# Late weight pieces' transfers as steps of a hand-written order, and all three step lists laid anew

## The reference

```python
# graph convolution on _gn(x)                            steps of
prod = einsum(lhs(x), rhs(x));  E = softmax(V_e @ sigmoid(prod + b_e))     # M prod Epre Eexp Erep
prod2 = einsum(lhs2(x @ E), rhs2(x @ E))                                   # lr p2
S = softmax(V_s @ sigmoid(prod2 + b_s))                                    # sp rv
out = sum_k einsum(cheb[k], S, x) @ Theta[k]                               # Y st o
y = relu(conv1x3(relu(out), tw) + tb + einsum(x, rw) + rb)                 # tc
x = x + layernorm(y) * gamma + beta                                        # xb z1 z2 z3
# linear attention on _ln_t(t), causal, 16 heads
num = cumsum(phi(k) v^T) phi(q);  den = cumsum(phi(k)) . phi(q) + eps      # k q v S V, kt kv dent
t = t + (num / den) @ Wo.T + bo                                            # rd at wo
# mixture of experts on _ln_t(t): 16 experts of width 64, 2 of 4 groups, top 4, and a shared FFN of width 512
w = top4(sigmoid(xf @ router_w.T) + correction_bias);  w /= sum(w)         # lg r1 r2 r3 r4 cb
t = t + sum_e w_e * down_e(silu(gate_e xf) * up_e xf) + shared_ffn(xf)     # gu h w dn
```

## Time and profile before

| | us |
|---|---|
| three runs | 930.55, 930.71, 933.21 |
| median | 930.71 |
| the profiled execution | 933.24 |
| its span on the core | 931.3 |
| TensorE busy | 892.2 |
| VectorE busy | 623.1 |
| ScalarE busy | 445.6 |
| POOL busy | 228.6 |

### The profile page before, as it was taken

One profiled execution on the slowest core, in us unless ns is written; L12 is line 12 of the kernel. 1 busy time (PEld: TensorE's weight loads), 2 busy tenths in 40 slices (PEclk: granted clock), 3 DMA queues, 4 the chain that ended last, 5 costly groups with the idle time before them and its releaser, 6 DMA issues.

```text
span 931.3 us, 19454 instructions
## 1 busy us (share of the span) xinstructions
PE 892.2 (96%) x7824; PEld 787.5 (85%) x7824; DVE 623.1 (67%) x1637; ACT 445.6 (48%) x845; POOL 228.6 (25%) x198
## 2 busy tenths in 40 slices
PE   5998788999999999999999999999999999999997
PEld 3676666998988989889898989888898898998997
DVE  6456876887697468864797467963788547864522
ACT  3443444552574436743565526744466424732432
POOL 2013200123311224112421234112241134122232
...
DMA packets 37961, 39.21 MB, mean 42 GB/s; under 512 B 5232, under 2 KB 34416, under 8 KB 37872
## 3 DMA queue, kind: packets, MB, share of 16 engines
...
...
## 4 chain that ended last, share of the span: by engine, by line
PE 83%; DVE 8%; ACT 4%; issue 2%; DMA 1%; POOL 0%; SPq 0%; POOLq 0%; DVEq 0%; ACTq 0%
PE ring L1365 9%; PE d_ps L521 5%; PE g_ps L521 4%; PE d_ps L523 4%; PE d_ps L522 4%; PE g_ps L523 4%; PE u_ps L523 4%; PE g_ps L522 4%; PE u_ps L522 4%; PE u_ps L521 4%; PE ring L1233 4%; PE num L1262 3%; PE ring L521 3%; PE ring L1348 3%; PE ring L523 3%; PE ring L522 3%
## 5 line engine op out<-in xcount | busy, mean ns | idle before, releaser
L707 POOL TENSOR_TENSOR hl<-hb,hh 128x512 fp32r<-128x512 f32 x96 | 126.0, 1313 | 424.4 <-ACT hh L838 424.4
L838 ACT ACTIVATE hh<-hb 128x512 fp32r<-128x512 f32 x96 | 60.7, 632 | 143.5 <-DVE hb L1205 119.0
L1200 DVE TENSOR_TENSOR hb<-sl,u_ps 128x512 f32<-128x512 f32 x88 | 60.3, 685 | 93.3 <-issue 37.6
L521 PE MATMUL d_ps<-hh,down_h 128*128 128x256 f32 x384 | 116.6, 304 | 2.7 <-POOL hl L707 2.7
L522 PE MATMUL d_ps<-hl,down_h 128*128 128x256 f32 x384 | 107.8, 281 | 0.0
L523 PE MATMUL d_ps<-hh,down_l 128*128 128x256 f32 x384 | 107.6, 280 | 0.0
L521 PE MATMUL g_ps<-normed_h,gate_h 128*128 128x256 f32 x352 | 105.7, 300 | 1.1 <-DVE hb L1200 0.8
L1087 DVE TENSOR_TENSOR shared<-ring,constants 128x512 f32<-128x512 f32 x128 | 79.4, 683 | 34.1 <-PE ring L1233 34.1
L523 PE MATMUL g_ps<-normed_h,gate_l 128*128 128x256 f32 x352 | 99.2, 282 | 0.0
L523 PE MATMUL u_ps<-normed_h,up_l 128*128 128x256 f32 x352 | 99.0, 281 | 0.0
L522 PE MATMUL u_ps<-normed_l,up_h 128*128 128x256 f32 x352 | 98.8, 281 | 0.0
...
## 6 DMA issues: line engine op xcount, KB each, us to landing
weights_over_hidden<-weights_by_expert SPq DMA_DIRECT2D x128, 128.0 KB, 3.0
...
```

Of the source, the lines that this page charges most:

```text
L521: eng.matmul(ps, wh, xh, start=start, stop=False, **how)
L707: pool.tensor_tensor(hl[:, j % 2, :], hb, hh[:, j % 2, :].bitcast(F32), ALU.subtract).then_inc(*ffn_pool.mark(p, f"lo{j}"))
L838: act.activation(hh[:, j % 2, :], hb, ACT.Copy).then_inc(*ffn_act.mark(p, f"hi{j}"))
L1200: dve.tensor_tensor(hb, sl, gate_up(p, j)[1][:, :], ALU.mult).then_inc(*ffn_dve.mark(p, f"h{j}"))
```

## The change

The transfers of pieces 4 to 13 become steps load4 to load13 of a chain of their own. SP issues pieces 0 to 3 before its walk as before, and each later one where its step stands in the list; the wait for pair 1's z3 stays ahead of piece 4. All three lists are laid anew; the work in the steps is the same. Lines below the lists move by 2 to 8 (L1365 becomes L1373).

```diff
@@ -110,41 +110,43 @@
-ONCE = ("warm", "high", "low")
+EARLY_PIECES = 4
+CHAINS["load"] = [f"load{i}" for i in range(EARLY_PIECES, 14)]
+ONCE = ("warm", "high", "low", "load")
...
 OPENING = """
-    0:gn 0:hot0 0:xg 0:hot1 0:xT0 0:hot2 1:gn 0:M 0:xT1 0:high0 1:xg 0:high1 0:Y0 1:xT0 2:gn 0:high2 0:prod
...
+    0:gn 0:hot0 1:gn 0:hot1 0:xg 0:load4 1:xg 0:hot2 0:low0 0:high0 0:xT0 0:M 0:xT1 0:hot3 0:hot4 0:Y0 1:xT0
...
 BODY = """
-    +1 tok0 tok1 lg +1 gn +1 nrm +3 xg +1 r1 xl0 xl1 xT0 +1 r2 M +2 k0 xT1 k1 r3 +2 Y0 +1 prod v1 silu r4
-    Epre cb Eexp q0 v0 kt q1 +2 Erep dent +1 kv lr rd +2 S00 +2 V00 S01 +1 p2 at0 +1 V01 S10 +2 sp0 +1 rv0 +1
-    sp1 st0 +1 rv1 Y1 +2 st1 +1 o0 +2 V10 +1 S11 +2 o1 tc0 tc1 xb +1 z1 +1 V11 +2 at1 z2 +2 wo0 wo1 +2 tk0
-    exp tk1 +5 nrm2 z3 +1 xn0 xn1 +1
+    +1 tok0 tok1 lg +1 gn +2 nrm xg +1 r1 +3 xl0 xT0 xl1 M r2 +2 xT1 k0 k1 +2 Y0 +1 prod v1 r3 silu Epre r4
+    cb Eexp q0 v0 kt q1 +2 Erep dent kv +1 lr +1 rd +1 S00 +2 V00 S01 +1 p2 +1 at0 V01 S10 +2 sp0 rv0 sp1 +2
+    st0 +1 rv1 Y1 xb +2 st1 +1 o0 o1 +1 tc0 tc1 +2 z1 +2 V10 S11 +1 V11 +4 at1 z2 wo0 +1 wo1 +2 tk0 tk1 +2
+    nrm2 +3 z3 +1 xn0 xn1 +1 exp
 """
 
 CLOSING = """
...
-    7:r3 +1 7:silu 7:r4 +1 7:cb +30 7:exp +17
...
+    7:silu 7:r4 +1 7:cb +18 7:exp +32
@@ -546,7 +548,7 @@
 
         for half in (1, 0):
             feed_forward(gateT, gate_h, gate_l, 2 * wide, 0, half)
-        EARLY_PIECES = len(PIECES)
+        assert EARLY_PIECES == len(PIECES)
         for half in (1, 0):
             feed_forward(gateT, gate_h, gate_l, 2 * wide, 1, half)
             for k in range(2):
@@ -582,7 +584,11 @@
             for k in range(3):
                 sp.dma_start(cheb_s[:, k], cheb[k].rearrange("(c m) n -> m c n", m=P)).then_inc(load["graph"], 16)
             sp.dma_start(wo_s[:, :, :], woT.rearrange("(c j) k -> j c k", j=P)).then_inc(load["graph"], 16)
-            for i in range(len(PIECES)):
+            for i in range(EARLY_PIECES):
+                sp.dma_start(PIECES[i][3], PIECES[i][0]).then_inc(piece_loaded[i], 16)
+
+            def load_piece(i):
+
                 if i == EARLY_PIECES:
                     sp.wait_ge(tail_dve.of(1), tail_dve.at(1, "n30"))
                     sp.wait_ge(tail_pool.of(1), tail_pool.at(1, "n31"))
@@ -627,6 +633,8 @@
                                  source.unsqueeze(0).to_broadcast([64, 2, L])).then_inc(over_loaded[r % 2], 16)
 
             for p, name in PROGRAM:
+                if name in CHAINS["load"]:
+                    load_piece(int(name[4:]))
                 if name == "xb" and ROOMS - 1 <= p < PAIRS - 1:
                     prefetch(p + 1)
                 if name in ("out0", "out1"):

```

More of the change, by code:

```diff
@@ L119 @@
 OPENING = """
-    0:gn 0:hot0 0:xg 0:hot1 0:xT0 0:hot2 1:gn 0:M 0:xT1 0:high0 1:xg 0:high1 0:Y0 1:xT0 2:gn 0:high2 0:prod
[L121 to L133, removed]
+    0:gn 0:hot0 1:gn 0:hot1 0:xg 0:load4 1:xg 0:hot2 0:low0 0:high0 0:xT0 0:M 0:xT1 0:hot3 0:hot4 0:Y0 1:xT0
+    2:gn 0:prod 1:M 0:load5 1:xT1 0:Epre 0:Eexp 1:Y0 2:xg 1:prod 0:Erep 1:Epre 0:hot5 0:high1 0:hot6 0:hot7
@@ new lines @@
+    0:lr 2:xT0 1:Eexp 1:Erep 0:p2 1:lr 0:low1 0:sp0 0:load6 0:high2 0:rv0 1:p2 0:sp1 0:st0 1:sp0 0:rv1 2:M
+    0:low2 0:Y1 1:rv0 0:load7 2:xT1 1:sp1 0:st1 0:o0 0:high3 1:st0 0:o1 2:Y0 0:load8 0:xb 0:tc0 0:tc1 1:rv1
+    2:prod 1:Y1 0:z1 0:z2 2:Epre 1:st1 1:o0 0:z3 2:Eexp 1:xb 1:o1 1:tc0 0:tok0 1:tc1 0:tok1 1:z1 0:nrm 0:hot8
+    0:hot9 2:Erep 2:lr 1:z2 0:xl0 0:xl1 2:p2 1:z3 0:k0 0:low3 0:k1 0:v1 0:q0 0:v0 0:kt 0:q1 0:hot10 2:sp0
+    0:hot11 0:dent 0:hot12 0:high4 0:high5 0:high6 0:kv 0:rd 0:S00 0:V00 0:load9 0:high7 0:high8 2:rv0 0:S01
@@ new lines @@
+    0:hot13 0:low4 0:at0 0:hot14 0:V01 0:high9 0:S10 0:hot15 0:hot16 0:high10 0:hot17 2:sp1 0:high11 2:st0
+    0:hot18 0:V10 0:hot19 0:low5 0:S11 0:hot20 0:load10 2:rv1 0:low6 0:hot21 0:hot22 0:hot23 0:low7 0:V11
+    0:at1 0:low8 2:Y1 0:wo0 0:wo1 0:tk0 0:load11 0:tk1 0:nrm2 2:st1 2:o0 0:xn0 0:xn1 0:load12 0:low9 1:tok0
+    1:tok1 0:low10 2:o1 1:nrm 0:low11 0:lg 0:r1 +2 0:load13 1:xl0 +1 1:xl1 +1 0:r2 0:high12 0:high13 0:r3
+    1:k0 0:silu +1 0:r4 1:k1 0:cb +2 1:v1 1:q0 1:v0 0:low12 1:kt +2 1:q1 2:tc0 +2 2:xb 0:low13 2:tc1 +1
@@ L134 @@
+    1:dent 1:kv +1 1:rd +2 1:S00 +3 0:exp 1:V00 +1 1:S01 +4 1:at0 1:V01 1:S10 +3 1:V10 2:z1 1:S11 +3 1:V11 +1
+    1:at1 +1 2:z2 1:wo0 1:wo1 +1 2:z3 +4 1:tk0 1:tk1 +5 1:nrm2 +3 1:xn0 1:xn1 +3 1:exp
 """
 BODY = """
-    +1 tok0 tok1 lg +1 gn +1 nrm +3 xg +1 r1 xl0 xl1 xT0 +1 r2 M +2 k0 xT1 k1 r3 +2 Y0 +1 prod v1 silu r4
-    Epre cb Eexp q0 v0 kt q1 +2 Erep dent +1 kv lr rd +2 S00 +2 V00 S01 +1 p2 at0 +1 V01 S10 +2 sp0 +1 rv0 +1
-    sp1 st0 +1 rv1 Y1 +2 st1 +1 o0 +2 V10 +1 S11 +2 o1 tc0 tc1 xb +1 z1 +1 V11 +2 at1 z2 +2 wo0 wo1 +2 tk0
@@ L140 @@
-    exp tk1 +5 nrm2 z3 +1 xn0 xn1 +1
+    +1 tok0 tok1 lg +1 gn +2 nrm xg +1 r1 +3 xl0 xT0 xl1 M r2 +2 xT1 k0 k1 +2 Y0 +1 prod v1 r3 silu Epre r4
+    cb Eexp q0 v0 kt q1 +2 Erep dent kv +1 lr +1 rd +1 S00 +2 V00 S01 +1 p2 +1 at0 V01 S10 +2 sp0 rv0 sp1 +2
+    st0 +1 rv1 Y1 xb +2 st1 +1 o0 o1 +1 tc0 tc1 +2 z1 +2 V10 S11 +1 V11 +4 at1 z2 wo0 +1 wo1 +2 tk0 tk1 +2
+    nrm2 +3 z3 +1 xn0 xn1 +1 exp
 """
 CLOSING = """
-    +1 7:tok0 7:tok1 +2 7:nrm +1 6:lg +1 7:xl0 7:xl1 6:r1 6:r2 +2 7:k0 +1 6:r3 6:silu +1 6:r4 6:cb 7:k1 7:v1
@@ L145 @@
-    7:q0 +1 7:v0 +2 7:kt 7:q1 +3 7:dent 7:kv 7:rd +3 7:S00 +3 7:V00 +1 7:S01 +2 7:at0 +2 7:V01 7:S10 +4 7:V10
-    7:S11 +2 7:V11 +2 7:at1 7:wo0 +3 7:wo1 +2 7:tk0 7:tk1 +5 7:nrm2 7:xn0 7:xn1 +3 7:lg +1 7:r1 +3 7:r2 +3
-    7:r3 +1 7:silu 7:r4 +1 7:cb +30 7:exp +17
+    +1 7:tok0 7:tok1 6:lg 7:nrm 6:r1 +1 6:r2 7:xl0 7:xl1 6:r3 +1 6:silu +1 6:r4 6:cb 7:k0 7:k1 7:v1 +2 7:q0
+    7:v0 7:kt +2 7:q1 +3 7:dent 7:kv +3 7:rd 7:S00 +3 7:V00 7:S01 +1 7:at0 +2 7:V01 7:S10 +4 7:V10 7:S11 +3
+    7:V11 7:at1 +3 7:wo0 +1 7:wo1 +4 7:tk0 7:tk1 +2 7:nrm2 +4 7:xn0 7:xn1 +2 7:lg 7:r1 +4 7:r2 +4 7:r3 +1
```

## The result

The changed kernel took 924.04 us (median of 8 runs, 922.38 to 925.0), the kernel before 931.13 in the same count (926.55 to 933.21): a ratio of 0.9928, 95% interval 0.9908 to 0.9948, some 7 us less. 923.5 was forecast. The profiled execution took 922.38, with a span of 920.4; against the 931.3 of before that is 10.9 less, more than the medians differ, since the execution profiled before was among the longest of its kernel and this one is the shortest of its own.

What follows compares the result with a forecast made beforehand. TensorE, busy 107.72 of 108 us a turn, was taken as the body's bound; the opening has waits and lower clock. Opening -3.2, body -2.5 and closing -1.5 sum to -7.2, giving 923.5 us on the median, range 919 to 927.9.

Steps and rivals of the forecast that it cites:

- Step 1: Opening's first steps: early hot matmuls cost +1.5 us, the middle of -0.4 (higher clock returns) and +3.5 (it does not).
- Steps 2 and 3: Opening: -0.8 us from steps removed ahead of 0:Y1, -1.8 from hot7 and hot8 no longer delaying 1:Y1.
- Step 4: Opening, gap before 2:lr: hot8 and hot9 in it keep the higher clock level behind it, -1.0 us.
- Steps 5 and 6: Pair 0: attention -2.1 us from fewer VectorE splits among score masks; FFN +1.0 us because kt waits for VectorE.
- Step 7: Body: 44 changes between rounded and plain operands become 42, -0.28 us a turn.
- Step 8: Body: tk0 behind wo no longer waits for VectorE's second x2 sum, -0.06 us a turn.
- Step 9: Body: ScalarE's table loads move behind nrm2, removing TensorE's wait for ScalarE, -0.3 us a turn.
- Step 10: Body: tok1's transposes wait for POOL's n31, +0.15 us a turn.
- The slower one: Body: VectorE's z1 ahead of S11's masks makes V11 wait, up to 2.72 us a turn, 938.2 us; chance 0.07.
- The stalls move: Body: savings come back as waits at tok1 and dn7; only changes of kind count, 928.8 us; chance 0.15.
- The opening gains nothing: Opening: waits only change names; body and closing alone give -4.0, 926.7 us; chance 0.18.
- the room on the weight loads: Body: order alone closes the weight loads' 11.9 us gap a turn, 59 us in five, some 864; chance 0.02.

Runs made afterwards that it cites:

- e2: Changed kernel with the opening of the kernel before, its transfers placed as in e1; changed body and closing kept: 929.16 us, ratio 0.9982 to before.
- e4: Changed kernel without the matmuls hot3 to hot7, which nobody reads: 927.0 us, ratio 0.9963 to the kernel before.
- f2: e4 with the wait ahead of 2:lr filled with unread matmuls as in f1: 926.12 us, ratio 0.9961 to the kernel before.
- f1: Changed kernel with hot8 and hot9 moved into the wait ahead of 2:lr, six more unread matmuls behind them: 924.46 us, ratio 0.9932 to before.
- h1: g2 with the wait ahead of 2:lr filled by eight unread matmuls: 931.51 us, ratio 1.0024 to the kernel before.
- e1: Lists of the kernel before, with only the ten late transfers made steps: 932.59 us, ratio 1.0007 to before.
- g2: e1 with only the early matmuls hot3 to hot7 moved to where the changed kernel has them: 931.77 us, ratio 1.0013 to before.
- h2: Lists before, transfers as steps, with only the wait ahead of 2:lr filled by eight unread matmuls: 930.51 us, ratio 1.0014 to before.
- g1: f1 with four more TensorE waits in the opening filled with unread matmuls: 923.13 us, ratio 0.9924 to the kernel before.
- f3: Changed kernel with o0, V10 with S11, and o1 with tc apart again in the body, xb behind tc: 924.43 us, ratio 0.9936 to before.
- f4: Changed kernel with exp between tk0 and tk1 again and nrm2 five FFN steps behind them: 924.81 us, ratio 0.9937 to before.
- e3: Changed kernel with only the body of the kernel before put back, changed opening and closing kept: 926.8 us, ratio 0.9966 to before.

## Why the prediction was right, and where it was not

The total held, 923.5 against 924.04, and so did the body's sum in the trace. That the total is so close is in part luck. By the medians the opening gave 5.1 where 3.2 was said, and body and closing, by e2, some 2 where 4.0 was said; the two errors cancel. And the opening's steps gave what they gave for reasons that were mostly not mine.

**Step 1, first steps (+1.5): wrong in sign.** I took the middle between the hots' price and the clock's return. They cost the path little: Y0 came 1.1 later, not 2.4, and 0:lr no later. Behind it 0:sp0 was done at 40.7 instead of 44.2: 3.5 us gained, beyond my end of -0.4. Against a profile of the same first steps without hots (e4) the gain is 1.6 at the end of 0:sp0, and none at 1:Y1. In another such profile (f2) 0:sp0 ends 2.1 us later than in e4: which level these steps have differs between executions. I also took TensorE for busy in four fifths of the 11.6 us ahead of 0:sp0's end; the trace of before has it busy throughout (5.00 of 5.00 us from 30 to 45).

**Steps 2 and 3 (-0.8 and -1.8): not there.** From 0:sp0 to 0:Y1 the profiles differ by 1.5, and 1.3 of it is the clock in sp0. From 0:Y1 to 1:Y1 it is 24.2 us, 0.3 longer than before. 1:Y1 waited for its own chain all the same, as the end of 0 said: the 1.0 us of hots in front became 0.8 us more of waiting for ScalarE.

**Step 4 (-1.0): the place right, the mechanism not.** hot8 and hot9 ahead of the gap did not keep the clock: it still fell, to 0.53. But it was back before k, and from 2:lr to 0:S00 it is 20.2 us instead of 22.8, -2.6. k shows most of it, before:

```profile
107.74 0.47 PE L521 MATMUL ring<-normed_h,wqkv_h 128*128 128x512 f32 x1 [1.24 <-DVE normed_l L1047]
...
112.17 0.28 PE L521 MATMUL ring<-wqkv_h,normed_h 128*128 128x256 f32 x1
```

and now:

```profile
103.29 0.47 PE L523 MATMUL ring<-normed_h,wqkv_h 128*128 128x512 f32 x1 [0.29 <-DVE normed_l L1055]
...
106.14 0.28 PE L523 MATMUL ring<-wqkv_h,normed_h 128*128 128x256 f32 x1
```

The first twelve matmuls of k take 2.85 us instead of 4.43, 1.6 less by the clock, and the wait ahead of them is 0.9 shorter by the order of steps. f1, e4 and h1 show how much of this stretch hangs on the moment at which the level comes back.

**Steps 5 and 6 (-2.1 and +1.0): a quarter of the one, nothing of the other.** From 0:S00 to lg of pair 0 it is 42.8 us instead of 43.4; from there to lg of pair 1 81.4 instead of 81.5. (To and from the first FFN matmul the two look like -1.0 and +0.4, but 0.4 of each is xl0 changing sides.) The wait for S00's masks, 2.6, is as long as before: taking lows from behind them did not shorten it.

So the opening is earlier by 6.9 in the profiles, at lg of pair 0, and 5.1 by the medians of e2 and the changed kernel, where -3.2 was said. It is not the transfers (e1), not the early matmuls alone (g2, 0) and not the gap (h2, 0). The new order without early matmuls (e4) is 2 us below e2 (their intervals overlap), with them another 3. That taking out five early matmuls costs 3 us in the new order, and that moving them to these places gives none in the old one, was measured; why stays open. The two are not quite the same test, since the old order has these five too, at other places, and no run leaves them out there. In the profiles the difference is the clock in k, which falls in the old order behind a wait of 1.4 us (g2) or 1.7 (h1) and not in the changed kernel, behind 0.3; but f1 waits 1.3 us there and keeps its level, and g1 waits as long and loses it, so the length of that wait alone does not decide it.

**The body (-0.49 a turn): -0.48.** Step 7 said -0.28, f3 shows -0.13; the term that failed is the return of 0.31 behind o0, 0.19 of which belongs to the o matmul. Step 8 said -0.06: tk0 now starts 0.12 behind the last matmul ahead of it, -0.15. Step 9 said -0.3, f4 shows -0.37. Step 10 said +0.15, 0.18 stands in the waits; since f4 does not have that wait, its -0.37 already has the 0.18 in it, and the parts found do not simply add up. The sum is right and the terms are not: errors in them cancel. A wait that the forecast did not name, for the spread weights in the fourth turn, came with the new body: that turn takes 107.53 where the others take 107.2.

**The closing (-1.5): 1.2.** In the closing no product waits for the spread weights any longer, and the smaller wait for POOL, 0.5, is gone, as said. e3 has 1.2 from lg of pair 5 on. The waits for VectorE are as long as before, 0.9 instead of 0.8, at other places.

**The rivals.** The slower one did not come: no V11 waits in any turn, so the masks behind z1 were done in time. "The stalls move" came true in part, 0.18 a turn at tok1. "The opening gains nothing" is refuted by e2. For the room on the weight loads: they are busy for 95.86 of 107.20 us now, 11.3 less than all, where it was 11.9 of the 108.00 of the earlier trace rows; the new order took some 0.5 of it. The Trainium skill, "Perfetto Trace Analysis", section "Identifying the Most-Contended Engine", names that share, beside the share of the peak floating-point rate, as the measure of headroom; by it the room is still there. No run here shows that it can be filled.
